# Splitting the softmax maxima into three bf16 parts on VectorE in place of GpSimd, in a two-layer attention tower

## What is computed

```python
h = tok(x, W)
h = h + attn0(layernorm(h))      # softmax(q k^T * scale + bias) v, projected
h = h + ffn0(layernorm(h))       # routed and shared layers
h = h + attn1(layernorm(h))      # softmax(q k^T * scale) v, projected
h = h + moe1(layernorm(h))       # top 2 of 8 experts
```

## Time and profile before

| | us |
|---|---|
| median of 3 runs | 4194.81 (4194.46 to 4199.51) |
| the profiled execution | 4199.6 |
| its span, first to last instruction | 4197.8 |
| TensorE matmuls busy | 3900.1 (93%) |
| VectorE busy | 2903.8 (69%) |
| ScalarE busy | 2638.1 (63%) |
| GpSimd busy | 857.9 (20%) |
| mean granted TensorE clock | 0.972 |

### The profile page before, as it was taken

One profiled execution on the slowest core, in us unless ns is written; L12 is line 12 of the kernel. 1 busy time (PEld: TensorE's weight loads), 2 busy tenths in 40 slices (PEclk: granted clock), 3 DMA queues, 4 the chain that ended last, 5 costly groups with the idle time before them and its releaser, 6 DMA issues.

```text
span 4197.8 us, 62363 instructions
## 1 busy us (share of the span) xinstructions
PE 3900.1 (93%) x21508; PEld 1308.8 (31%) x21508; DVE 2903.8 (69%) x4955; ACT 2638.1 (63%) x4768; POOL 857.9 (20%) x1263
## 2 busy tenths in 40 slices
PE   6988999999999999999999999999999999999897
PEld 3223333332333323333333333323323333332222
DVE  4866767676776777757677776777767677677672
ACT  0656666666666666666666666666666666666564
POOL 4122212121211312212122121312212122121211
PEclk7999999999999999999999999999999999999998
DMA  5113201222112122111222112122111222111100
GB/s 103 37 31 56 39 21 31 51 40 42 34 34 41 31 42 49 36 25 31 42 48 42 33 35 41 31 42 49 33 27 31 42 49 42 30 31 28 23 10 6
DMA packets 119067, 156.36 MB, mean 37 GB/s; under 512 B 24847, under 2 KB 66575, under 8 KB 118717
## 3 DMA queue, kind: packets, MB, share of 16 engines
q1 hardware_dynamic: 118753, 152.38, 18.8%
HBM read 120.01 MB, written 29.36 MB: 36 GB/s over the span
## 4 chain that ended last, share of the span: by engine, by line
PE 68%; ACT 7%; POOL 7%; issue 6%; DVE 6%; DMA 2%; SPq 1%; POOLq 0%; ACTq 0%; DVEq 0%
PE acc L911 18%; PE side_st L897 18%; PE nat L885 15%; PE side_st L854 3%; DVE tile_max L1294 3%; PE side_st L750 2%; ACT hidden L1073 2%; POOL ln_s L1392 2%; ACT prob L1101 2%; PE side_st L840 2%; PE side_st L727 2%; PE side_st L807 1%; DMA q_rows<-max_rows 1%; ACT hidden L1019 1%; SPq L607 1%
## 5 line engine op out<-in xcount | busy, mean ns | idle before, releaser
L1294 DVE TENSOR_REDUCE tile_max<-nat 128x1 f32<-128x512 f32 x4096 | 2602.3, 683 | 1142.4 <-PE nat L885 1108.5
L1101 ACT ACTIVATE prob<-side_st 128x512 f32<-128x512 f32 x4096 | 2226.0, 600 | 1412.1 <-PE side_st L897 1373.7
L897 PE MATMUL side_st<-q_rows,k_rows 99*128 99x512 bf16 x4096 | 1578.4, 388 | 62.6 <-ACT prob L1101 32.3
L885 PE MATMUL nat<-k_rows,q_rows 96*128 96x512 bf16 x4096 | 1548.1, 389 | 35.8 <-DVE tile_max L1294 25.7
L911 PE MATMUL acc<-prob,v_padded 128*32 128x512 f32 x8192 | 1108.3, 613 | 6.0 <-ACT prob L1101 5.1
L897 PEld LDWEIGHTS side_st<-q_rows,k_rows 99*128 99x128 bf16 x4096 | 400.3, 99 | 1309.5 <-ACT prob L1101 903.9
L885 PEld LDWEIGHTS nat<-k_rows,q_rows 96*128 96x128 bf16 x4096 | 404.6, 99 | 529.8 <-DVE tile_max L1294 288.3
L1455 POOL TENSOR_SCALAR max_parts<-neg_max 128x16 bf16<-128x16 f32 x128 | 26.2, 205 | 1896.2 <-DVE neg_max L1301 1895.0
L911 PEld LDWEIGHTS acc<-prob,v_padded 128*32 128x32 f32 x8192 | 162.6, 108 | 376.7 <-ACT prob L1101 197.2
L840 PE MATMUL side_st<-ln_rows,w 64*128 64x512 f32 x512 | 140.1, 624 | 28.3 <-ACT hidden L1073 22.8
L1380 POOL TENSOR_SCALAR ln_s<-ln_s 128x8 f32<-128x8 f32 x64 | 12.9, 202 | 709.4 <-DVE ln_s L1202 705.7
(11 more groups left out here) (124 smaller groups left out, 2074.9 us busy)
## 6 DMA issues: line engine op xcount, KB each, us to landing
q_rows<-q_scratch SPq DMA_DIRECT2D x576, 64.0 KB
k_rows<-k_scratch SPq DMA_DIRECT2D x192, 192.0 KB
x_rows<-in_x SPq DMA_DIRECT2D x62, 512.0 KB, 6.5
q_scratch<-hidden SPq DMA_DIRECT2D x32, 384.0 KB
k_scratch<-hidden SPq DMA_DIRECT2D x96, 128.0 KB
group_weights<-in_routed SPq DMA_DIRECT2D x64, 129.0 KB, 2.1
q_rows<-max_rows SPq DMA_DIRECT2D x512, 3.0 KB
out_h<-out_rows SPq DMA_DIRECT2D x16, 256.0 KB, 2.1
```

Source lines behind the costliest of these rows:

```text
L885: eng.matmul(NAT[use % len(NAT)][:, :], QA[u][0:K_NAT, h, c:c + P], KA[u][0:K_NAT, h, kh * 512:kh * 512 + 512], start=True, stop=True)\
L897: eng.matmul(RING[TILE_BANK[n0 + n]][:, :], KA[u][0:K_ALL, h, t * P:t * P + P], QA[u][0:K_ALL, h, half * 512:half * 512 + 512], start=True ...
L1101: eng.activation(prob[:, n % TILES, :], RING[TILE_BANK[n0 + n]][:, :], ACT.Exp).then_inc(exp_done, 1)
L1294: eng.tensor_reduce(mx[:, q % 2, j // 8, j % 8 // 2, j % 2:j % 2 + 1], NAT[use % len(NAT)][:, :], AX.X, ALU.max).then_inc(nat_free, 1)
```

## The change

VectorE now makes the three parts itself, with four instructions directly behind the one that makes the maxima, each waiting for the one before it through a semaphore; `split_max` and its calls are gone from GpSimd. The rounding is a copy to bf16 where GpSimd had a multiplication by one. The wait for the DMAs that last read this half of the parts moves along; VectorE's wait for the parts of the round before is left out, since it now makes them itself.

```diff
             def super_max(n0, q):
                 v = over(n0, SUPER) + q
                 eng.wait_ge(nat_free, at(SUPER * (v + 1)))
-                eng.wait_ge(parts_ready, at(v - 1))
-                eng.tensor_reduce(neg_max[:, q % 2, :, :], mx[:, q % 2, :, :, :], AX.X, ALU.max, negate=True)\
-                    .then_inc(negm_ready, 1)
+                p, nm, rs = mparts[q % 2], neg_max[:, q % 2, :, :], mres[:, q % 2, :, :]
+                eng.tensor_reduce(nm, mx[:, q % 2, :, :, :], AX.X, ALU.max, negate=True).then_inc(negm_ready, 1)
+
+                eng.wait_ge(negm_ready, at(v + 1))
+                eng.wait_ge(maxrow_in[q % 2], at(DMA_MAX * (v // 2)))
+                eng.tensor_copy(p[:, :, 0, :], nm).then_inc(mchain, 1)
+                eng.wait_ge(mchain, at(3 * v + 1))
+                eng.tensor_tensor(rs, nm, p[:, :, 0, :], ALU.subtract).then_inc(mchain, 1)
+                eng.wait_ge(mchain, at(3 * v + 2))
+                eng.tensor_copy(p[:, :, 1, :], rs).then_inc(mchain, 1)
+                eng.wait_ge(mchain, at(3 * v + 3))
+                eng.tensor_tensor(p[:, :, 2, :], rs, p[:, :, 1, :], ALU.subtract).then_inc(parts_ready, 1)
...
-            def split_max(n0, q):
...
-                eng.tensor_scalar(p[:, :, 0, :], nm, 1.0, 0.0, ALU.mult, ALU.add).then_inc(mchain, 1)
...
-                if kind == "first":
-                    split_max(n0, 0)
...
-                    ahead = n + SUPER + LEAD
-                    q = ahead // SUPER
-                    if ahead % SUPER == SUPER - 1 and (kind != "last" or q < SUPERS):
-                        split_max(n0, q)
```

## The result

| | before | changed |
|---|---|---|
| median, us | 4195.88 (4 runs, 4194.46 to 4199.51) | 4163.18 (4 runs, 4161.06 to 4167.43) |
| span of the profiled execution, us | 4197.8 | 4159.3 |
| mean granted clock | 0.972 | 0.982 |
| VectorE busy, us | 2903.8 | 3023.2 |
| GpSimd busy, us | 857.9 | 749.9 |

The ratio is 0.9922, with a 95% interval of 0.9905 to 0.9939. The change made the kernel 0.8% faster, where I had forecast 0.5% slower. The time lies in the range, but on the other side of no change.

The account below looks back on a forecast made before the run. TensorE's matmuls were taken as the bound. Per pair 2.2 + 1.7 - 1.8 - 2.93 + 2.5 = +1.7 us, times 14 +24, about -3 elsewhere: median from 4194.8 to about 4215 us, range 4115 to 4250.

Parts of the forecast that it names:

- the queries/keys place: Where GpSimd splits queries and keys, 14 times: 3.66 us wait goes, net gain 1.8 us, and 2.93 with the clock.
- the tight rounds: Three of a pair's eight rounds, where VectorE's four added instructions delay TensorE: 1.7 us lost per pair.
- the hold at the queries/keys place: GpSimd's long instructions delay VectorE's second copy; nat comes 1.60 us later, piled-up work adds about 0.25.
- the first copy is held until 1369.75: Layer norm place: GpSimd's power holds VectorE's copy, starting a delay of 2.2 us per pair, plus 2.1 of clock.
- rival 1: VectorE isn't held by GpSimd anywhere; layer norm place comes out even, pair near -4.9 us: 4118 us, chance 0.15.
- my -3: Net change outside the 14 pairs, in the first five rounds and the ending: about -3 us.
- the layer norm place: Where GpSimd ends a layer norm, 14 times: 0.65 us wait goes, 2.85 us hold comes, 2.2 us lost.
- The one long wait with its low clock: In the first five rounds, one long wait for GpSimd goes with its low clock: about -7 us.
- the four tight rounds: In the first five rounds, four rounds where VectorE's added work delays TensorE, costing 0.5 us each.
- The place that I had 2 us worse, at 245 us: In the first five rounds, one place like the layer norm place, forecast to come out 2 us worse.
- The ending: The end of the kernel, counted with the first five rounds in a total of about -3 us.
- Rival 2: Only the subtractions are held by GpSimd, not the copies: 4165 to 4205 us, 4192 in the middle, chance 0.25.

Follow-up runs that it names:

- e2: Kernel before the change, GpSimd still splitting the maxima, but ahead of its split of queries and keys when both fall together: 4105.6 us, ratio 0.9778.
- e5: Kernel before the change, with VectorE also making the parts, into tiles nobody reads (added work alone): 4207.59 us, ratio 1.0026.
- e7: Changed kernel with the two copies to bf16 replaced by reductions over one element: 4156.02 us in one run.
- e9: Changed kernel with GpSimd's layer norm power replaced by one 128x840 addition of the same length, 1.65 us: 4213.63 us, ratio 1.0044.
- e11: Changed kernel with GpSimd's layer norm power replaced by eight additions of 128x8 in a row: 4168.96 us in one run.

## Why the prediction was wrong

**Right: the bound and the two places.** The turning matmul's wait is gone. The 6.6 us per pair at the queries/keys place, wait and low clock, are what e2 gave back (6.5). That the clock's half came along with the wait, and not as something of its own, is shown by the stretch at 1.00 and by e2.

**Right: the tight rounds.** 170 ns and 34 ns were taken, 174 and some 33 measured (L1305 to L1309 start every 0.21 us), the next reduction 0.94 us behind the maxima for my 0.91. A pair lost 1.70 us for 1.7. The 77 ns that the cycle formula in the Trainium skill's "VectorE: DVE Perf Modes" (section on the TRN2 errata) gives is refuted by 174. Alone, in e5, the same rounds cost the same.

**Right: the hold at the queries/keys place**, read from one instruction at 127.5 us. The copy is held to 0.95 and 2.06 us, `nat` comes at 4.35 behind the maxima for my 4.40, the turning matmul at 6.33 for the 6.37 that follow from it. The Trainium skill's rule in "SBUF — State Buffer" (section "SBUF: two separate sides"), with the list in its section "Who interferes with whom" of which of VectorE's instructions share the port, agrees with the copies, the subtractions and, by e7, with reductions being free of it.

**Wrong: "the first copy is held until 1369.75" by GpSimd's power.** This one step carried 4.3 us per pair (2.2 and 2.1 of clock), 60 us in all, more than the whole distance of 52 us between 4215 and 4163. The power takes 1.65 us, and I read its length as time at the port, while all four of VectorE's instructions took 174 to 178 ns under it. Had I left the step out and taken the chain unheld, as rival 1 does for this place (+0.16), the sum would have been +1.7 - 4.3 + 0.2 = -2.4 us per pair, for -2.3 measured, and 14 of them with my -3 would have given 4158. The Trainium skill's "SBUF — State Buffer", in the same section "SBUF: two separate sides", says that whoever starts first keeps the pair for the whole instruction. The additions of e9 and e11 agree with it, with VectorE's end 0.03 us behind theirs; for the power the trace speaks against it, from 0.27 us behind its start on. e9 shows that the rest of the step was right in its order: under an addition of that length it happens as written, and costs 3.7 us against the kernel before where I had put 4.3 with the clock.

The row that I took as the contrast, the maxima at 0.19 us "also while GpSimd's power runs", was no contrast at all. The maxima are a reduction, and e7 shows reductions unheld even under 128x1024; and the power held nothing here. The row fitted every theory. What I had no row for was a copy or subtraction under a power, and that should have widened the middle of my forecast: I gave the case that the long additions hold and the power doesn't no chance of its own.

**Too small: what lies outside the pairs.** I had -3 us for it. The -38.5 us of the span less 14 x (-2.3) leave some -6. The one long wait with its low clock gave 6.8 for my 7, and the four tight rounds ahead of it cost 1.9 for my 2. The place that I had 2 us worse, at 245 us, came out 3.3 better. That is the same step again: the power held none of VectorE's chain there either, and a wait of 1.4 us went with the low clock behind it. The ending, which I had at about nothing, cost 2.8.

**The rivals.** None of them was the case. Rival 2's range, 4165 to 4205, comes nearest with its lower end, and only by luck: the copies are held as well. Rival 1 was right at the layer norm place (0.16 us worse, 0.1 measured) and wrong at the queries/keys place, where 16-element instructions were held in 14 pairs of 14.

**What stays open.** Why the power lets VectorE through. That it has few elements is not enough, since additions on as few hold it. Whether every power does so, or whether this one is at the port only in its first 0.27 us, was not run: a power on many elements would have to be put in its place. And I can't say from these runs what makes the clock fall for 3.4 us in one pair and not at all in the next behind the same 1.6 us of idle time.

## What to carry to other kernels

When work is moved from GpSimd to VectorE, look at what GpSimd will be doing at that moment: copies and two-input instructions on SBUF waited for its instructions, even with 16 elements themselves, while reductions and work from PSUM went on. Don't take the hold from an instruction's duration alone: the power lasted 1.65 us and held nothing that was seen. Before moving work to another engine because a wait ends at the old one, look at what stands ahead of it in the old queue. Here a change of order on GpSimd (e2) was worth 90 us and the move 33, since the short job had only been standing behind a long one. And a chain with a reader close behind it belongs in one piece right behind its source: spread out, it was 91 us slower.

## What the runs showed of the hardware

- A 128x16 copy or subtraction on VectorE takes 174 ns and can follow its producer through a semaphore every 0.21 us. Held by GpSimd it took up to 2.08 us, and ended 0.03 us behind the end of GpSimd's instruction, be that an addition of 128x8 or of 128x840, or a bf16 rounding of 128x1024.
- Under GpSimd's long instructions, in the changed kernel, the copy out of PSUM (L1287) took some 0.273 us and the instruction with one input in PSUM (L1210) some 0.415, as they do elsewhere.
- A waiting VectorE instruction gets in between two of GpSimd's, also where these follow one another without a wait (0.65 us for L1312 under L1450, and not 2.6).
- The granted clock fell to 0.50, the lower level of 1.2 GHz, for 6.8 us behind one gap of 3.7 us, and mostly for 3.4 us where the same place had two gaps of 1.5 and 2.1. In the changed kernel, with one gap of 1.6 us, it fell in 4 pairs of 14.
